# One-hot turns by TensorE issued in twos at six places of a batch instead of in bursts of six and five

## What is computed

```python
xW = (x @ W).reshape(n, heads, out_ch)
alpha_s = jnp.sum(xW * a_src, axis=-1)
alpha_d = jnp.sum(xW * a_dst, axis=-1)
e = jax.nn.leaky_relu(alpha_s[src] + alpha_d[dst], SLOPE)
m = jax.ops.segment_max(e, dst, num_segments=n)
w = jnp.exp(e - m[dst])
z = jax.ops.segment_sum(w, dst, num_segments=n)
out = jax.ops.segment_sum(xW[src] * (w / z[dst])[:, :, None], dst, num_segments=n)
```

## Time and profile before

| | |
|---|---|
| median of three runs | 2513.81 us (2513.65 to 2521.13) |
| span of the profiled execution | 2493.9 us |
| what lies around the span (median less span) | 19.9 us |
| layer 1, batches 0 to 39 | 114.4 to 786.0 us, 16.7 us a batch in its middle |
| layer 2 | 869.3 to 1551.9 us, 17.1 us a batch |
| layer 3 | 1664.1 to 2469.8 us, 20.2 us a batch |
| busy share of the span | PE 71%, DVE 64%, POOL 60%, ACT 55% |
| granted TensorE clock, mean | 0.770 of 2.4 GHz |

### The profile page before, as it was taken

One profiled execution on the slowest core, in us unless ns is written; L12 is line 12 of the kernel. 1 busy time (PEld: TensorE's weight loads), 2 busy tenths in 40 slices (PEclk: granted clock), 3 DMA queues, 4 the chain that ended last, 5 costly groups with the idle time before them and its releaser, 6 DMA issues. The chain is left out here.

```text
span 2493.9 us, 43223 instructions
## 1 busy us (share of the span) xinstructions
PE 1779.5 (71%) x9241; PEld 1123.8 (45%) x9241; DVE 1586.0 (64%) x4409; ACT 1366.9 (55%) x5004; POOL 1504.0 (60%) x1648
## 2 busy tenths in 40 slices
PE   6267767676766277776776767558888887878874
PEld 5144445444444144444444444335555555555542
DVE  4466666666668155555554556657777777877777
ACT  3255565556556144334344446536676667767666
POOL 3666666666657556656656663626666666766663
PEclk9576676767678566667777677768999989989886
DMA  6644444445531334434433531323433433433331
GB/s 175 160 124 121 115 122 123 118 117 156 144 84 58 97 105 109 111 106 110 112 106 110 164 101 37 113 59 100 114 108 109 117 112 107 114 107 108 107 89 52
DMA packets 130635, 274.39 MB, mean 110 GB/s; under 512 B 39700, under 2 KB 65273, under 8 KB 130366
## 3 DMA queue, kind: packets, MB, share of 16 engines
q0 software_dynamic: 64128, 181.33, 26.9%
q1 hardware_dynamic: 61564, 86.45, 11.6%
q10 hardware_dynamic: 4699, 3.86, 0.6%
HBM read 255.00 MB, written 17.20 MB: 109 GB/s over the span
## 5 line engine op out<-in xcount | busy, mean ns | idle before, releaser
L1271 POOL DMA_INDIRECT rows<-table,index_all x1320 | 1287.8, 976 | 833.2 <-PE bank L1775 383.8
L1775 PE MATMUL bank<-rows,onehot 128*128 128x264 f32 (+1 forms) x2640 | 1089.8, 529 | 290.1 <-ACT rows L1481 156.3
L839 DVE TENSOR_TENSOR sums<-sums,bank 128x264 f32 (+1 forms) x1320 | 555.7, 421 | 465.8 <-PE bank L1775 202.8
L1481 ACT ACTIVATE rows<-rows,wgt 128x33 f32<-128x33 f32 (+2 forms) x3120 | 809.6, 344 | 1.2 <-issue 1.1
L1775 PEld LDWEIGHTS bank<-rows,onehot 128*128 128x128 f32 x2640 | 557.9, 247 | 461.7 <-issue 204.7
L1433 ACT CAST onehot<-bank 128x768 f32<-128x768 bf16 x240 | 177.7, 742 | 301.5 <-remote 174.4
L1489 ACT ACTIVATE prod<-bank 128x512 f32<-128x512 f32 x240 | 133.6, 557 | 244.5 <-PE bank L1787 126.2
L1794 PE MATMUL bank<-late,onehotT 128*128 x1320 | 202.1, 291 | 1.1 <-DVE prod L848 1.1
L848 DVE TENSOR_TENSOR prod<-prod,bank 128x512 f32<-128x512 f32 x240 | 152.4, 635 | 50.3 <-remote 27.4
L857 DVE TENSOR_REDUCE dots<-prod 128x16 f32<-128x512 f32 x240 | 151.7, 632 | 0.5
L1696 PE MATMUL bank<-identb,onehotT 128*128 128x128 bf16 x1320 | 138.3, 251 | 16.6 <-issue 10.0
(11 more groups left out here) (208 smaller groups left out, 2018.0 us busy)
## 6 DMA issues: line engine op xcount, KB each, us to landing
locb<-loc_d SPq DMA_DIRECT2D x120, 352.0 KB
rows<-table,index_all POOLq DMA_INDIRECT x1320
flags<-flags_d SPq DMA_DIRECT2D x508, 27.5 KB
table<-rows SPq DMA_DIRECT2D x25, 136.0 KB, 1.8
table<-rows SPq DMA_DIRECT2D x25, 134.0 KB
late<-table SPq DMA_DIRECT2D x1, 3300.0 KB
table<-rows SPq DMA_DIRECT2D x25, 129.5 KB, 2.3
late<-table SPq DMA_DIRECT2D x1, 3212.5 KB
```

Source lines behind the costliest of these rows:

```text
L839: done(v.tensor_tensor(a, a, sum_bank(l, t, s)[:, 0:VV], ALU.add), "add")
L1271: g.indirect_dma_start(out=rows[:, t.u, s, 0:ROW[l]], out_offset=None, in_=table[l], in_offset=bass.IndirectOffsetOnAxis(ap=index_all[:, t ...
L1481: i = a.activation(r, r, ACT.Copy, scale=wgt[:, t.u, h * B + s:h * B + s + 1])
L1775: done(m.matmul(sum_bank(l, t, s)[:, 0:VV], onehot[:, t.u, s, :], rows[:, t.u, s, 0:VV], start=True, stop=True), "agg")
```

## The change

The two bursts of turns become six small groups: slots 0 and 1, 2 and 3, 4 and 5 of the first bank, 6 and 7, 8 and 9, and 10 of the second. `hotP` now has six places a layer. What the groups wait for and what they signal stays at the two banks: the first group of a bank waits for the bank's last copy, the last one signals. ACT's copies move: in layer 1 from s = 3 and 4 to 3 and 6, in layer 2 from 0 and 1 to 3 and 6, in layer 3 from 2 and 6 to 3 and 8. Ahead of each layer's loop the turns stay together. No matmul, copy or semaphore step is added or removed.

```diff
+TURNS = tuple((g, j, min(j + 2, hi)) for g, (lo, hi) in enumerate(HOTS) for j in range(lo, hi, 2))
...
-         link=5, exp=7, weights=8, hotT=(3, 4), copy=8,
-         endsT=2, cols=4, weightsT=7, hotP=(1, 2), adst=6, scoresT=9),
+         link=5, exp=7, weights=8, hotT=(3, 6), copy=8,
+         endsT=2, cols=4, weightsT=7, hotP=range(0, 6), adst=6, scoresT=9),
...
-         link=2, exp=7, weights=7, hotT=(0, 1), copy=7,
-         endsT=1, cols=4, weightsT=7, hotP=(0, 1), adst=5, scoresT=8),
+         link=2, exp=7, weights=7, hotT=(3, 6), copy=7,
+         endsT=1, cols=4, weightsT=7, hotP=range(0, 6), adst=5, scoresT=8),
...
-         link=3, exp=6, weights=8, hotT=(2, 6), copy=9,
-         endsT=1, cols=4, weightsT=7, hotP=(1, 5), adst=3, scoresT=8),
+         link=3, exp=6, weights=8, hotT=(3, 8), copy=9,
+         endsT=1, cols=4, weightsT=7, hotP=(0, 1, 2, 5, 6, 7), adst=3, scoresT=8),
...
+                    for i, turn_ in enumerate(TURNS):
+                        if turn_[0] == g:
+                            hot_turn(t, i)
+
+                def hot_turn(t, i, l=l):
+
+                    kk = l * K + t.k
+                    g, first, end = TURNS[i]
+                    lo, hi = HOTS[g]
+                    if i == 0:
                         need(pe, "hot", kk + 1)
-                    need(pe, "hotT", 2 * kk + g - (1 if l < 2 else 0))
-                    lo, hi = HOTS[g]
-                    for s in range(lo, hi):
+                    if first == lo:
+                        need(pe, "hotT", 2 * kk + g - (1 if l < 2 else 0))
+                    for s in range(first, end):
                         r = m.transpose(ps_hotb[l][g][:, (s - lo) * P:(s - lo + 1) * P], onehotT[:, t.u, s * P:(s + 1) * P],
                                         identb[:, :])
-                    done(r, "hotp")
+                    if end == hi:
+                        done(r, "hotp")
...
                         if s in AT[l]["hotP"]:
-                            hot(n2, AT[l]["hotP"].index(s))
+                            hot_turn(n2, AT[l]["hotP"].index(s))
```

More of the change, by code:

```diff
@@ L1688, in hot @@
                 def hot(t, g, l=l):
+                    for i, turn_ in enumerate(TURNS):
+                        if turn_[0] == g:
+                            hot_turn(t, i)
+                def hot_turn(t, i, l=l):
                     kk = l * K + t.k
-                    if g == 0:
+                    g, first, end = TURNS[i]
+                    lo, hi = HOTS[g]
+                    if i == 0:
                         need(pe, "hot", kk + 1)
-                    need(pe, "hotT", 2 * kk + g - (1 if l < 2 else 0))
-                    lo, hi = HOTS[g]
-                    for s in range(lo, hi):
+                    if first == lo:
+                        need(pe, "hotT", 2 * kk + g - (1 if l < 2 else 0))
+                    for s in range(first, end):
                         r = m.transpose(ps_hotb[l][g][:, (s - lo) * P:(s - lo + 1) * P], onehotT[:, t.u, s * P:(s + 1) * P],
                                         identb[:, :])
-                    done(r, "hotp")
+                    if end == hi:
+                        done(r, "hotp")
                 def adst(t, l=l, H=H):
```

## The result

The change took 2492.43 us (median of 8 runs, 2480.56 to 2511.91) against 2516.77 us for the kernel before beside it (2513.65 to 2521.94), a ratio of 0.991 with a 95% interval of 0.989 to 0.994. Further comparisons split this result in two.

The account below looks back on a forecast made before the run. The prediction took each batch as bound by a loop through POOL: gathers and waits for PE's slots 3 and 7. Span 2493.9, +3 for layer 2, 0 for layers 1 and 3, and 19.9 around it gave 2517, called 2518 us; range 2457 to 2552.

Follow-up runs that it names:

- IV: Comparison on one chip, unchanged kernel beside the change and others: 2490.40 us before, 2491.21 us with the change, ratio 1.000 (0.997 to 1.003).
- V: Comparison on another chip, unchanged kernel beside the change and others: 2516.03 us before, 2492.02 us with the change, ratio 0.990 (0.987 to 0.993).

## What to carry to other kernels

Where one engine issues gathers in a row, look for results of TensorE that come true together some 2.5 us after the last of them began, and look at more than one batch; put the head of a dependent chain ahead of TensorE's bulk work there, and check which result falls into the hold in its place, since the gain is gone if that is the chain's next link. Before a change is priced against a trace, set that execution's own time beside the median: if they differ by more than the gain looked for, they may come from two places where the kernel runs differently, and the verdict in one is not the verdict in the other. A kernel with two rhythms shows in the spread of its runs (31 us against 8 in the first comparison) and in waits that are bunched at two values.

## What the runs showed of the hardware that was not expected

- Results of TensorE that are queued while another engine issues gathers in a row are in many batches seen by others only when the run of gathers is over: 2 to 3.1 us after its last gather began, be it a run of four, seven or eleven, after up to 9.0 us (the second burst of layer 2 behind eleven). Some get through ahead of that: behind eleven gathers the ends came 5.0 us late but mostly ahead of the last gather. `cols` was caught 4.1 us into a run; ends with one turn ahead got through at 7.0 us. What in the chip makes it, and what exactly decides who is caught, is open.
- It doesn't depend on the bytes: 3.36 or 54.00 MB in a layer give the same waits. The last packet of a run ends 2.5 us after its last gather began with whole rows and 2.1 with short ones, averaged over layer 2's records, and the wait is the same, so the wait doesn't end with the last packet. With the short rows a gather has 32 packets and not 48; fewer were not tried.
- The Trainium skill (DMA: Bandwidth & Descriptors, Anatomy of one DMA — SWDGE (gpsimd) path) gives 2.0 us plus the bytes over 436 GB/s for one transfer of this kind. Worked out from this as an estimate, 8 and 133 KB take 2.0 and 2.3 us. The traces agree within 0.2 us: 2.1 and 2.5 us from the start of a run's last gather to its last packet's end.
- The same program waits 1.95 us for slot 3 of layer 1 in IV and 2.08 in V, and takes 2490 or 2516 us. That the longer hold is also what keeps the change in the early-hold rhythm fits its four traces, but was not tested apart.
